# One-core language-model tower: half of the graph vectors by one-hot products over a streamed word table, with the first stage unrolled

## What is computed

```
def _vgcn(word_emb, gv_ids, adj, W, b):
    ev = word_emb[gv_ids]                       # (B, 128, 192)
    H = jnp.einsum('bgh,bhd->bgd', adj, ev)
    g = H.mean(axis=1)
    return jax.nn.relu(g @ W.T + b)             # (B, 16)
emb = word_emb[input_ids] + pos_emb             # (B, 128, 192)
graph = concat([_vgcn(cooc), _vgcn(het), _vgcn(isg)], axis=1), the same for every position
y = concat([emb, graph], axis=2) @ W_proj.T + b_proj
y = layernorm(y) * ln_gamma + ln_beta           # then a second layernorm feeds the convolution
```

## Time and profile before

| What | us |
|---|---|
| median of 3 runs | 1190.51 (1187.79 to 1192.35) |
| the profiled execution's own time | 1180.91 |
| its span, first to last instruction | 1178.8 |
| mean granted clock of TensorE | 0.798 of full speed |

### The profile page before, as it was taken

One profiled execution on the slowest core, in us unless ns is written; L12 is line 12 of the kernel. 1 busy time (PEld: TensorE's weight loads), 2 busy tenths in 40 slices (PEclk: granted clock), 3 DMA queues, 4 the chain that ended last, 5 costly groups with the idle time before them and its releaser, 6 DMA issues. The chain is left out here.

```text
span 1178.8 us, 22895 instructions
## 1 busy us (share of the span) xinstructions
PE 929.6 (79%) x7666; PEld 892.2 (76%) x7666; DVE 612.3 (52%) x2089; ACT 521.0 (44%) x1211; POOL 671.1 (57%) x592
## 2 busy tenths in 40 slices
PE   1578587777686779494893599999999999999993
PEld 0478587777686779494892489988988998999992
DVE  2125454434354546537968455654655655655551
ACT  1102121213112122355774467666766675667671
POOL 6455555647465650002440267776777787888874
PEclk9986665656555656697555599999999999999997
DMA  6323443626161625392068254466466446444442
GB/s 211 82 76 132 134 158 103 199 65 223 49 216 47 223 77 153 113 288 77 1 192 235 79 146 62 58 138 173 58 156 156 62 60 156 59 62 63 62 53 30
DMA packets 99385, 138.08 MB, mean 117 GB/s; under 512 B 13284, under 2 KB 81031, under 8 KB 97255
## 3 DMA queue, kind: packets, MB, share of 16 engines
q0 software_dynamic: 39552, 53.26, 23.9%
q1 hardware_dynamic: 58742, 73.39, 20.3%
q10 hardware_dynamic: 1008, 10.34, 2.4%
HBM read 98.13 MB, written 38.82 MB: 116 GB/s over the span
## 5 line engine op out<-in xcount | busy, mean ns | idle before, releaser
L884 ACT ACTIVATE Hs<-bank,U 128x256 bf16<-128x256 f32 x426 | 209.7, 492 | 174.5 <-PE bank L716 149.9
L475 POOL DMA_INDIRECT ev_g<-in_word_emb,ids_i x192 | 192.6, 1003 | 159.6 <-PE bank L574 105.4
L511 POOL DMA_INDIRECT out<-Hs,id_s x142 | 235.4, 1658 | 75.1 <-issue 74.8
L1205 DVE TENSOR_TENSOR Hs<-Hs 128x512 bf16<-128x512 f32 x213 | 147.7, 693 | 189.2 <-ACT Hs L885 165.3
L885 ACT ACTIVATE Hs<-bank,U 128x256 f32<-128x256 f32 x426 | 211.6, 497 | 0.0
L731 PE MATMUL bank<-U,Hs 128*128 128x192 bf16 x852 | 210.0, 247 | 0.3 <-issue 0.3
L733 PE MATMUL bank<-U,Hs 128*128 128x192 bf16 x852 | 208.8, 245 | 0.0
L732 PE MATMUL bank<-U,Hs 128*128 128x192 bf16 x852 | 208.6, 245 | 0.0
L502 POOL DMA_INDIRECT blob<-xtab_d,id_g x142 | 145.6, 1025 | 103.9 <-DVEq L1189 51.4
L712 PE MATMUL bank<-blob,U 128*128 128x256 bf16 x426 | 116.9, 274 | 16.5 <-issue 14.5
L573 PE MATMUL bank<-cs,ev_g 128*128 128x1 f32 x384 | 94.6, 309 | 43.8 <-issue 43.8
(11 more groups left out here) (183 smaller groups left out, 1704.0 us busy)
## 6 DMA issues: line engine op xcount, KB each, us to landing
adj_s<-in_adj SPq DMA_DIRECT2D x48, 256.0 KB
ev_g<-kpad_d SPq DMA_DIRECT2D x24, 512.0 KB, 5.8
U<-blob_d SPq DMA_DIRECT2D x14, 771.0 KB
wst<-in_wsrc SPq DMA_DIRECT2D x8, 1344.0 KB
blob_d<-blob ACTq DMA_DIRECT2D x7, 1443.0 KB
U<-blob_d SPq DMA_DIRECT2D x14, 672.0 KB
xtab_d<-U SPq DMA_DIRECT2D x4, 1552.0 KB, 9.0
out<-Hs SPq DMA_DIRECT2D x4, 1536.0 KB, 11.6
```

Source lines behind the costliest of these rows:

```text
L475: pool.indirect_dma_start(ev_g[:, p, j, b, :], None, t["word_emb"], bass.IndirectOffsetOnAxis(ap=ids_i[:, 1 + j, i * Q + b:i * Q + b + 1], ...
L511: pool.indirect_dma_start(out, bass.IndirectOffsetOnAxis(ap=id_s[:, 2 * q + h:2 * q + h + 1], axis=0), yo[:, q % RX, h, :], None, compute_ ...
L884: f(hh[w][:, d, :], ps, ACT.Gelu, bias=bi[:, d:d + 1])
L1205: last = v.tensor_tensor(hl[w][:, c:c + 2, :], hf[w][:, c:c + 2, :], hh[w][:, c:c + 2, :], ALU.subtract)
```

## The change

It does the following.

- **Graph vectors of batches 32 to 63** (quads 8 to 15) are no longer gathered. For these 96 vectors (32 batches, 3 graphs) a matrix `C` is built that holds, for each word of the table, the sum of the column means whose index names that word. The table is laid over 128 partitions with 240 words each (TV); C is built in two halves of 120 words per partition (TH), each by 24 units (`build(u)`, 4 vectors each). A unit takes 4 f32 matmuls of 120 columns on PE, whose operands are one-hot tiles that DVE makes (`one_hots(u)`: one 480-element and four 128-element instructions, three buffers), and one 480-element copy on ACT (`evacuate(u)`), which writes with a step of 384 bytes.
- **The table is streamed**: 30 chunks (NE) of 8 words per partition (786 KB), with three buffers (`load_chunk`, 61 DMAs on SP), each used by 8 f32 matmuls of 192 columns (`stream(s)`), 240 in all, that add up the 96 vectors in one bank. Features of the far batches come from 2 transposes and 12 small matmuls.
- **Column means** of all 16 quads are made ahead of everything: DVE adds the four rows held by a partition (`row_sums`, 768 and 384 elements per quad), PE multiplies three times per quad with 128 columns (`column_sums`), in four sets with a turn and two copies for each.
- **POOL** issues 96 gathers fewer, and those that remain wait for earlier ones to land (each graph's four for the group two before them).
- **The layernorm** moves its first scaling to ACT (`first_norm`, 4 instructions a quad); DVE does two 768-element instructions for gamma and beta, and the second layernorm's reciprocal root is taken for groups of 4, 4, 4, 2, 1 and 1 quads. `project` has one set of banks rather than two.
- **The loops** over quads are unrolled on all engines, in an order written out by hand. On SP all adjacency loads come first, then the chunks, with the loads of experts 1 to 6 after chunks 2, 7, 12, 17, 21 and 25.

The core of the diff (indented less than in the file):

```diff
+TV = 240
+TH = TV // 2
+VROWS = V - 127 * TV
+BU = 4
+NU = ND // BU
+HOTS = 3
+ET = 8
+NE = TV // ET
+EB = 3
+LN_GROUPS = (4, 4, 4, 2, 1, 1)
...
+def load_chunk(s):
+    k, t0 = s % EB, s * ET
+    if s >= EB:
+        sp.wait_ge(streamed, s - EB + 1)
+    full = 128 if t0 + ET <= VROWS else 127
+    for p0, p1 in ((0, 112), (112, full)):
...
+def next_expert(e):
+    sp.wait_ge(w_out, 16 * e)
+    load_expert(e)
+for n in range(NQ):
+    if n >= 2:
+        sp.wait_ge(adj_used, n - 1)
+    load_adj(set_quad(n), n % 2)
+    if n == 7:
+        load_expert(0)
+for s in range(NE):
+    load_chunk(s)
+    if s in (2, 7, 12, 17, 21, 25):
+        next_expert((2, 7, 12, 17, 21, 25).index(s) + 1)
+next_expert(E - 1)
...
+    if 0 < i <= NGQ:
+        pool.wait_ge(ev_in[1 - p][1], 16 * Q * ((i - 1) // 2 + 1))
                 after(pool, emb_t, i - 1)
...
+    if i < NGQ:
+        after(pool, gvec, i - 1)
+        for j in range(GRAPHS):
+            if j == 1:
+                pool.wait_ge(emb_in[p], 16 * Q * (i // 2 + 1))
+            if j == 2:
+                pool.wait_ge(ev_in[p][0], 16 * Q * (i // 2 + 1))
...
+def column_sums(k):
+    after(pe, c_ready, k - 1)
+    for n in range(4 * k, 4 * k + 4):
+        pe.wait_ge(summed, n + 1)
+        for j in range(GRAPHS):
...
+def build(u):
+    pe.wait_ge(hots, u + 1)
+    after(pe, evac, u - 1)
+    for i in range(BU):
+        last = mm(bank[6 * (u % 2)][:, i * TH:(i + 1) * TH], hot_hi[:, u % HOTS, i, :], hot_lo[:, u % HOTS, i, :], start=True, stop=True)
+    last.then_inc(built, 1)
+def stream(s):
+    if s % (NE // 2) == 0:
+        pe.wait_ge(evac, NU * (2 * s // NE + 1))
+    pe.wait_ge(e_in[s % EB], 16 * chunk_loads(s))
+    for tt in range(ET):
+        at_t = s * ET + tt
+        rows = 128 if at_t < VROWS else 127
+        last = mm(bank[7][0:ND, 0:D], C[0:rows, at_t % TH, :], E_s[0:rows, s % EB, tt, :], start=at_t == 0, stop=at_t == TV - 1)
+    last.then_inc(streamed, 1)
...
+build(5)
+pe.wait_ge(pos_done, 1)
+enter(0)
+for u in range(6, 9):
+    build(u)
+graph_features(0)
+for u in range(9, 12):
+    build(u)
+project(0)
+for u in range(12, 18):
+    build(u)
+enter(1)
+for u in range(18, 21):
+    build(u)
+graph_features(1)
+for u in range(21, 24):
+    build(u)
+project(1)
+pe.wait_ge(kready, 2)
+for s in range(NE // 2):
+    stream(s)
+    if s in (2, 8):
+        enter(2 + s // 8)
+    if s in (4, 10):
+        graph_features(2 + s // 8)
+    if s in (6, 12):
+        project(2 + s // 12)
+for u in range(NU, 2 * NU):
+    build(u)
+    if u == 29:
+        enter(4)
+    if u == 32:
+        graph_features(4)
+    if u == 35:
+        project(4)
+for s in range(NE // 2, NE):
+    stream(s)
+    if s == 18:
+        enter(5)
+    if s == 20:
+        graph_features(5)
+    if s == 22:
+        project(5)
+enter(6)
+far_rows()
+graph_features(6)
+far_features()
+project(6)
+enter(7)
+graph_features(7)
+for i in range(NGQ, NQ):
+    turn_embeddings(i)
+    project(i - 1)
+project(NQ - 1)
...
+def evacuate(u):
+    act.wait_ge(built, u + 1)
+    if u == NU:
+        act.wait_ge(streamed, NE // 2)
+    m = (u % NU) * BU
+    f(C[:, :, m:m + BU], bank[6 * (u % 2)][:, 0:BU * TH].rearrange("p (m t) -> p t m", m=BU), ACT.Copy).then_inc(evac, 1)
...
+for i in (2, 3):
+    enter(i)
+    split_hi(i - 1)
+    features(i)
+    store_expert(act, i - 1)
+    first_norm(i)
...
+split_hi(4)
+enter(5)
+store_expert(act, 4)
+features(5)
+split_hi(5)
+first_norm(5)
+store_expert(act, 5)
+split_hi(6)
+act.wait_ge(streamed, NE)
...
+def row_sums(k):
+    for n in range(4 * k, 4 * k + 4):
+        dve.wait_ge(adj_in[n % 2], 16 * GRAPHS * (n // 2 + 1))
+        a = adj_s[:, n % 2, :, :, :]
+        v.tensor_tensor(a[:, :, 0:2, :], a[:, :, 0:2, :], a[:, :, 2:4, :], ALU.add)
+        fence()
+        v.tensor_tensor(a[:, :, 0, :], a[:, :, 0, :], a[:, :, 1, :], ALU.add).then_inc(summed, 1)
+def one_hots(u):
+    h, m0, slot_u = u // NU, (u % NU) * BU, u % HOTS
+    after(dve, built, u - HOTS + 1)
+    v.tensor_tensor(hot_lo[:, slot_u, :, :], repeat(iota_f[:, h * TH:(h + 1) * TH], 1, BU), repeat(hot_at[:, 2, m0:m0 + BU], 2, TH), ALU.is_equal)
+    for i in range(BU):
+        m = m0 + i
+        c = c_set[:, 2 * (m // SR), m % SR:m % SR + 1]
+        last = v.tensor_scalar(hot_hi[:, slot_u, i, :], iota_f[:, 0:128], hot_at[:, 1, m:m + 1], c, ALU.is_equal, ALU.mult)
+    last.then_inc(hots, 1)
...
+def hidden_rows(i):
+    p, g = i % 2, ln_group(i)
+    at_i = (i - sum(LN_GROUPS[0:g])) * Q
+    dve.wait_ge(normed1, i + 1)
+    h = Hs[:, i * Q:(i + 1) * Q, :]
+    v.tensor_tensor(ys[:, p, :, :], ys[:, p, :, :], repeat(gamma[:, :], 1, Q), ALU.mult)
+    fence()
+    v.tensor_tensor(h, ys[:, p, :, :], repeat(beta[:, :], 1, Q), ALU.add)
...
+    n = LN_GROUPS[g] * Q
+    if at_i + Q == n:
+        b = slice((i + 1) * Q - n, (i + 1) * Q)
+        rsqrt(n, ln2[:, 0, b], mv2[:, 0:n, 1], EPS_LN)
...
+filter_argument(0)
+far_places()
+row_sums(0)
+row_sums(1)
+filter_argument(1)
+dve.wait_ge(c_ready, 1)
+for u in range(0, 3):
+    one_hots(u)
+row_sums(2)
+row_sums(3)
+position_bias()
+for u in range(3, 6):
+    one_hots(u)
+filter_taps()
...
+first_moments(0)
+split_lo(0)
+for u in range(15, 21):
+    one_hots(u)
+hidden_rows(0)
+for u in range(21, 24):
+    one_hots(u)
+first_moments(1)
+for u in range(24, 27):
+    one_hots(u)
+hidden_rows(1)
+for i in (2, 3):
+    split_lo(i - 1)
+    first_moments(i)
+    hidden_rows(i)
+split_lo(3)
+for u in range(27, 39):
+    one_hots(u)
+first_moments(4)
+for u in range(39, 45):
+    one_hots(u)
+hidden_rows(4)
+for u in range(45, 48):
+    one_hots(u)
+split_lo(4)
+first_moments(5)
+split_lo(5)
+hidden_rows(5)
+split_lo(6)
+first_moments(6)
+for i in range(7, NQ):
+    first_moments(i)
+    hidden_rows(i - 1)
+hidden_rows(NQ - 1)
```

More of the change, by code:

```diff
@@ L531, in _ @@
             mm = nc.tensor.matmul
[L533 to L539, removed]
@@ L592, in project, with enter @@
                 last.then_inc(proj, 1)
[L594 to L599, removed]
-                    graph_vectors(it, i, p)
-                    graph_features(i)
-                    project(i, p)
-            column_means(1, 0, 0)
-            steps(pe, NQ // 2, pair, last=1)
+            def enter(i):
+                turn_embeddings(i)
+                graph_vectors(i)
@@ new lines, in _ @@
+            enter(0)
+            for u in range(6, 9):
+                evacuate(u)
+            features(0)
+            for u in range(9, 15):
+                evacuate(u)
+            split_hi(0)
+            first_norm(0)
+            for u in range(15, 18):
+                evacuate(u)
+            enter(1)
+            for u in range(18, 21):
+                evacuate(u)
+            features(1)
+            for u in range(21, 24):
+                evacuate(u)
+            store_expert(act, 0)
@@ new lines, in _ @@
+            first_norm(1)
+            for i in (2, 3):
[4 more added lines that the diff above has]
+                first_norm(i)
+            split_hi(3)
+            for u in range(NU, 30):
+                evacuate(u)
+            store_expert(act, 3)
+            enter(4)
+            for u in range(30, 33):
+                evacuate(u)
+            features(4)
+            for u in range(33, 39):
+                evacuate(u)
@@ new lines, in _ @@
+            first_norm(4)
+            for u in range(39, 2 * NU):
+                evacuate(u)
+            split_hi(4)
[7 more added lines that the diff above has]
+            act.wait_ge(streamed, NE)
+            f(g_far[:, :], bank[7][0:ND, 0:D], ACT.Copy).then_inc(far_out, 1)
+            enter(6)
+            act.wait_ge(far_turn, 1)
+            f(gt_far[:, :, :], bank[6][:, 0:2 * ND].rearrange("p (c m) -> p c m", c=2), ACT.Copy).then_inc(far_t, 1)
@@ new lines, in _ @@
+            features(6)
+            act.wait_ge(far_feat, 1)
+            f(f_far[D1:PG, :], bank[0][D1:PG, 0:2 * SB], ACT.Relu, bias=gbias[D1:PG, :]).then_inc(far_ready, 1)
+            enter(7)
+            first_norm(6)
+            features(7)
+            store_expert(act, 6)
+            normal(0)
+            act.wait_ge(far_ready, 1)
+            for i in range(NGQ, NQ):
+                embedding_copy(i)
+                far_copy(i)
+                first_norm(i - 1)
+                for n in {8: (1, 2), 9: (3,), 10: (4,), 11: (5, 6), 12: (7,), 14: (8, 9), 15: (10,)}.get(i, ()):
+                    normal(n)
+                if i == 13:
+                    split_hi(7)
@@ L813, in turn @@
+            first_norm(NQ - 1)
+            for n in range(11, NQ - 1):
+                normal(n)
             def turn(it, s):
```

345 lines of the change are left out of this document (221 added, 124 removed).

## The result

| | before | after |
|---|---|---|
| median of the runs beside each other, us | 1190.03 (1187.79 to 1192.35, 4 runs) | 1256.53 (1249.69 to 1258.71, 4 runs) |
| the profiled execution, its span | 1180.91, 1178.8 | 1258.71, 1256.9 |
| mean granted clock | 0.798 | 0.830 |
| convolution's first matmul, us from the start | 489.6 | 568.2 |

The changed kernel is slower: ratio 1.0554, 95% interval 1.0516 to 1.0593, 66.5 us. All of the loss lies ahead of the convolution: 568.2 - 489.6 = 78.6 us between the two traces, whose spans differ by 78.1.

The account below looks back on a forecast made before the run. No engine full, so a chain bounds the kernel, graph vectors its long link. Stages 117 + 55 + 88 + 54 + 81 + 42 + 106 = 543 against 487.4, +56 us, giving 1246; range 1163 to 1288, own forecast 1205 to 1275.

Parts of the forecast that it names:

- A: Start, adjacency sums and first units, up to the end of `enter(0)`: 117 us, ends 104 and 126.
- B: From there to the first stream chunk, PE and DVE taking turns: 55 us, ends 50 and 60.
- C: Stream chunks 0 to 14 with two quads on PE and waits of 6 and 8: 88 us, ends 74 and 100.
- D: DVE's one-hot units up to 47, with layernorm work for quad 4 between: 54 us, ends 51 and 62.
- E: Stream chunks 15 to 29 on PE with waits of 7 and 18: 81 us, ends 57 and 92.
- F: After the stream, quads 6 and 7, far features and projections: 42 us, ends 38 and 48.
- G: DVE's tail over quads 7 to 15, DVE being the limit: 106 us, ends 100 and 114.
- The page against the row: Four stream waits: the skill page's DMA fit made them 17 us less, 1229 instead of 1246; the forecast kept the rows.
- R1: Rival, faster: graph vectors at upper clock save 44 us, stream waits (39) vanish, 1163 us; 0.25 for all that is faster.
- The issue idle time: PE's 84.7 us idle in the graph vectors without a visible wait, 5.3 us a quad, was taken to go.
- R3: Rival, slower still: idle time put down to issue returns in 8 quads, 42 us more, 1288 us; chance 0.10.
- The graph vectors as the long link: In the quads' loop before, a quad's 24 one-column matmuls take 10.3 us and are the chain's long link.

Follow-up runs that it names:

- experiment 3, `after_again`: The changed kernel, no edit, run again on another occasion beside the kernel before; 1220.29 us, ratio 1.1244.
- experiment 5: The changed kernel with one Newton step instead of three in the first square root of quads 7 to 15; 1212.96 us, ratio 1.1119 to the kernel before.
- experiment 4: The kernel before, no edit, one more traced run on a later occasion; 1080.04 us.
- experiment 1, `a_late`: The changed kernel with four expert loads later in SP's order; 1192.94 us, ratio 1.1042 to the kernel before.
- `a_late_rows`, experiment 9: The changed kernel with later expert loads and wide graph-vector matmuls in the 8 near quads; 1181.21 us, ratio 1.0893 to the kernel before.
- experiment 2: The kernel before with landing waits on POOL's gathers, with pair loops unrolled, and with both; 1083.56, 1080.87 and 1083.06 us.
- experiment 7: The kernel before, loops written out, graph vectors by 12 matmuls of 192 moving columns instead of 24 of one; 1053.71 us, ratio 0.9718.
- experiment 8: 56 gathers left out of the kernel before with loops written out (1084.49 us) and of its version with wide graph-vector matmuls (1005.35 us).
- `b_rows_fewer`: The kernel before with loops written out and wide graph-vector matmuls, 56 of the third graph's gathers left out; 1005.35 us, ratio 0.9303.

## Why the prediction was right, and where it was not

**The sum by stages.** All in us; the second column of measurements is from experiment 3's trace.

| Stage | forecast | first trace | experiment 3 |
|---|---|---|---|
| A, to the end of `enter(0)` | 117 | 120.2 | 105.9 |
| B, to the first chunk | 55 | 60.1 | 48.7 |
| C, chunks 0 to 14 | 88 | 99.6 | 98.0 |
| D, units 24 to 47 | 54 | 56.1 | 57.0 |
| E, chunks 15 to 29 | 81 | 86.1 | 86.1 |
| F, to quad 7's rows | 42 | 36.3 | 39.3 |
| G, DVE's tail | 106 | 107.6 | 107.6 |
| hand-over | 543 | 566.0 | 542.6 |

The mechanism was the one forecast: PE's account is nearly even, so the order of the work decides, and DVE's tail of 106 us stands open at its end. The tail was put to the test in experiment 5. PE's time up to the convolution shows the first part:

| Kernel, measurement | convolution at, us | PE busy | PE idle | of it put down to issue |
|---|---|---|---|---|
| before, first | 489.6 | 329.6 | 160.0 | 114.3 |
| changed, first | 568.2 | 344.8 | 223.4 | 14.6 |
| before, experiment 4 | 393.0 | 336.1 | 56.9 | 0 |
| changed, experiment 3 | 544.8 | 346.8 | 198.0 | 0 |

On balance PE's work grows by 11 to 15 us only. What grows is its idle time, by 141 us in the lower two rows, where none of it is put down to issue. In experiment 3 the largest waits are 51.9 us for the table, 43.4 for the row sums, 30.0 for ACT's copies of the embeddings, 25.9 for the end of the tail and 24.0 for the one-hots; the kernel before has 16.2 and 13.7 as its largest, for the end of the tail and for ACT's copies.

**How much of the number was luck.** The hand-over was put at 543 us and came at 566.0, 23 us later. The median comes within 10 us all the same, since 9.6 us were added for the distance between the traced run and the median, which the changed kernel doesn't show: its traced run is 2.2 us above its median. That the hand-over of experiment 3 agrees to 0.4 us is luck in part too, since C and A miss by about 10 each in opposite directions. And the graph vectors, told under G and F, were put too long, which made up for other terms that were put too short.

**A** was right for the first trace and 11 us too long for the other. A pair of sets was put at 8.4 us. In experiment 3 the first sums of the first three pairs start at 30.7, 39.0 and 47.7, 8.3 and 8.7 apart; the later sets are shorter than forecast, and so is the start, whose rows hold stalls of the first measurement: the first sums reach PE at 33.1 us there and at 21.8 in experiment 3.

**C** is the stage that was mis-sized most, by 12 us. The waits for chunks 8 and 13 were put at 6 and 8 and measured 8.9 and 10.5, with 1.6 and 0.7 more in front of others. The rest is some 2 us of issue idle time and PE's own work, 76.7 us where the sum had 74.

**E** had its waits at 7 and 18; they were 8.7 and 18.5. The cause, a store on ACT's queue behind `first_norm(5)`, agrees with experiment 1, where the longest wait is 5.6 us once the loads come later, and where the time fell with the waits.

**The page against the row.** The four waits came to 46.5 us, where the rows gave 39. The Trainium skill's fit ("DMA: Bandwidth & Descriptors", "Anatomy of one DMA — SWDGE (gpsimd) path") gave an estimated 22. The trace does not agree with it here. From the issue of the store to that of the load behind it are 11.9, 6.0, 5.7 and 5.2 us, where I had put 7; from there to the first matmul on the chunk are 11.2, 12.0, 13.9 and 11.9, where I had put 9.6. So what was mis-sized is the load and the chunk behind it. That they are slow because other transfers run beside them (the DMA share is 0.80 in stage C and 0.68 in E) is likely but not shown.

**G and F.** A quad of the tail was put at 9.7 us and takes 9.5. F was 6 us shorter. The term that was mis-sized most over the whole sum is in it: a quad's graph vectors at 10.3 us. Where they follow wide work they begin at the upper clock. In quad 2 the 24 matmuls take 8.0 us (188.99 to 196.98), the first half at 0.22 us each and the second at 0.43; in experiment 3 all but the last two ran at 0.22, and the whole took 5.8. Over the eight quads they take 5.4 to 8.0 us in the first trace, 55 in all where the sum had 82. The 10.3 was read off quad 0 of the kernel before alone; its quads 14 and 15 take 8.3 and 5.5 us. So more than half of what R1 expected of the clock did come, and other terms, the waits above all, were too small by as much and more. R1 had 5.5 us a quad to gain, 44 in eight, and all waits with them; `a_late` took most of the long waits away and gained some 22 us, and `a_late_rows`, which shortens the graph vectors too, gained 16 more. What remains are the waits listed in experiment 9, turns that PE takes with DVE, SP and ACT, and no clock shortens those.

**One-hots** on DVE were put at 1.6 us a unit, and that is what they take: neighbouring units start 1.59 us apart (104.67, 106.26, 107.86). D is 2 us longer than forecast, and B 5 longer in the first trace and 6 shorter in experiment 3. **ACT's copy** with its wide write step was costed at 0.6 and bounded at 1.1; it takes 0.57.

**The issue idle time** is the step that failed, though the total did not show it. I read it as belonging to the code (what is gathered is spread out now) and left 5.3 us a quad out of the sum. (The 10.3 us a quad under "Removed" hold none of it, as quad 0 has no such stall.) On the first occasion most of it did go: up to the convolution PE has 114.3 us of it before the change and 14.6 after, DVE 109.2 and 24.0, ACT 47.3 and 22.3. But the kernel before, unchanged, has 0, 5.2 and 2.0 us in experiment 4, and takes 1083 to 1084 us in all three sets; the changed kernel has 0, 2.9 and 0 in experiment 3. So the stalls need the circumstances of the first measurement, and why the changed kernel had fewer of them there isn't shown: the bounded gathers and the unrolled loops were tried only where there were none (experiment 2). R3, their return in full, did not come.

The Trainium skill, "Runtime: NRT & Kernel Launch", "Instruction fetch mechanics", would have the loops' taken branches cause stalls. The traces speak against that as the whole cause. In experiment 4 the loops are intact and the stalls are zero, and in the first trace PE stalls in quad 1 too, which stands in straight code ahead of the loop:

```profile
83.26 0.16 PE L573 MATMUL bank<-cs,ev_g 128*128 128x1 f32 x1 [1.96 <-issue]
86.04 0.16 PE L573 MATMUL bank<-cs,ev_g 128*128 128x1 f32 x1 [2.62 <-issue]
```

In that trace the 24 matmuls take 12.3 to 19.4 us in quads 1 to 13, and 8.3 and 5.5 in quads 14 and 15, which start at 441 and 459 us, while POOL issues its last gather at 444.9. That fits stalls beside gathers in flight, but the same gathers make none in experiment 4. What it was stays open. It matters for the verdict: with it the change costs 66 us, without it 136.

**What bounds the kernel.** The graph vectors as the long link was right and is now shown: making them wide gives 30 us (experiment 7), removing gathers alone gives nothing (experiment 8). "No engine is full, so the bound is a chain" was not: the engine behind it is PE, 94% busy at a clock of 0.64 where the stalls are absent. The first trace already had it, since in the loop PE waits for another engine for 18.2 us only (12.8 before L590 and 5.4 before L581, both for ACT), and the rest of its idle time is put down to issue.

## What to carry to other kernels

Before work is moved off a queue, leave a part of that work out and time it: 56 gathers fewer gave 0 us here, and 45 to 48 us once the engine that really bound the loop had been relieved. A busy share at a granted clock of 0.64, as here, can hide an engine that would give more to wider instructions: swapping the operands of a one-column matmul took 30 us off, with a few lines, where the large change lost 66 to 136. And idle time that no wait explains should be seen in a second trace, from another occasion, before a sum is built on its going.

## What the runs showed of the hardware that was not expected

- One program, 1190 us in the first measurement and 1083 to 1084 on three chips later, with TensorE's matmuls nearly as long (the mean of L574 is 312 and 328 ns) and the difference in idle time, most of it ahead of instructions that waited for nothing the profile shows, on PE, DVE and ACT alike.
- At the upper level of the clock, 2.4 GHz (granted clock 1.00 in both stretches below), an f32 matmul of one moving column against 128 held ones takes 0.22 us and one of 192 moving against 12 held ones 0.34 (24 records in 4.07 us, below). So one column costs two thirds of 192. PE's weight loads show where the time goes: from 163.4 to 168.0 us, with 128 held columns, they are busy for 4.60 of 4.60 us, and from 288.9 to 293.0, with 12 held, for 2.15 of 4.10. And 12 wide matmuls in place of 24 narrow ones save even with no gain of clock. PE's timeline in `b_rows_fewer` and, for the narrow ones, in `after_again`:

```profile
288.90 4.07 PE L575 MATMUL bank<-ev_g,cs 128*12 128x192 f32 x24
```

```profile
163.60 0.36 PE L660 MATMUL bank<-c,ev_g 128*128 128x1 f32 x2
163.82 0.36 PE L661 MATMUL bank<-c,ev_g 128*128 128x1 f32 x2
```

- DVE's compare with a scalar by partition lasts 347 ns for 128 elements, the same as the 192-element instruction in the earlier trace rows, yet four in a row take 1.11 us. The duration of one is not what it adds.
- ACT's copy out of PSUM with a write step of 384 bytes takes 571 ns for 480 elements, beside 597 for 512 contiguous ones; the step costs nothing that can be seen.
